# An eight-expert feed-forward layer: a loop of eight passes over token groups becomes one unrolled sequence

## The chip, the cores and the metric

The program runs on one core of a Trainium2 chip. The metric is the device time of one execution in microseconds (us). A core has a matrix engine (TensorE, PE in the profile; PEld are its weight loads), a vector engine (VectorE, DVE), a scalar engine (ScalarE, ACT), GpSimd (POOL) and SyncE (SP), which issues DMAs. The engines run their own instruction streams and meet at semaphores. PSUM is the memory that TensorE writes its results to, SBUF the working memory. Everything here is float32.

## The reference

The whole program is a stack of four attention-like layers and four feed-forward layers over a stream x of 4 x 1024 tokens with 128 features. Each adds its result to x. The change touches one of them, the feed-forward layer of the third block:

```python
x = x + L2_ffn(layernorm(x))

def L2_ffn(x):                                   # x: 4096 tokens x 128
    logits = x @ gate_w.T                        # 8 experts
    mult, sel = sparse_mixer_top2(logits, 0.01)  # two experts and two multipliers per token
    dense_w = zeros((T, 8)).at[rows, sel].set(mult)
    h1 = einsum('th,eih->eti', x, w1)            # 8 experts, 128 -> 256
    h3 = einsum('th,eih->eti', x, w3)
    act = silu(h1) * h3
    y = einsum('eti,ehi->eth', act, w2)          # 256 -> 128
    return einsum('eth,te->th', y, dense_w)

def sparse_mixer_top2(scores, eps):
    vals, idx = top_k(scores, 2)
    # for k = 1, 2: softmax over the scores s with (t_k - s) / max(|s|, t_k) <= 2 * eps
    # (for k = 2 without the first expert), and of it the value at idx_k
```

Every expert is computed for every token, and dense_w, zero for six of the eight experts, weights the results.

## The kernel before

The stream x lies in SBUF as X, [128, 32 tiles, 128]: 32 tiles of 128 tokens. The layer norm stage ahead of the layer writes its result turned, features on partitions, into XNT, [128, 32 * 128]. Stages follow one another; between two of them every engine waits at a barrier (`end_step`, which also has GpSimd clear the stage's semaphores).

`l2_ffn_stage` first loads and turns the weights (stages f2w0 to f2w2). Then comes stage f2s: `nc.Fori(0, TILES // G)` with G = 4, a loop in hardware of eight passes of four tiles each, with `end_step()` inside the loop. One pass has:

- ScalarE copies the pass's 512 columns of XNT into xs (L2279, with its table load), does two Exp for the routing (L2281, L2282) and 16 Tanh (L2287), from which silu is made.
- TensorE makes the logits of four tiles (L2293). Then for each expert e and each half k of its 256 hidden features it makes h1 (L2311) and h3 (L2313), products with 512 columns, and behind them the second product of the expert before, y(e-1) (L2302, eight products with 128 columns). In PSUM h1 and h3 have two buffers each and y has two.
- VectorE does the routing (L2323 to L2360), a chain of about 30 small instructions on 128x32 or 128x8 operands that ends with weight. After it, for each n = 2e + k, `hidden(n)` makes gated (L2365) and act (L2370). `gather(e-1)` adds weight times y(e-1) to acc (L2378 for the first expert, L2380 for the others), and at the end of the pass acc is added to X (L2392).

The waits that matter: TensorE may make h(n) when act(n-2) is done, and y(e) when act(2e+1) is done and y's buffer has been gathered. VectorE works in order, so that hidden(0) waits for the whole routing chain. `Chain` (called as `step`) makes an instruction signal a semaphore and VectorE wait for it, where the next one reads its result.

Each matmul in float32 stands in the trace as two instructions, so that L2302 has 16 for one expert. Two other stages have pieces of the same form: the last feed-forward layer's stage f3s makes the logits of 32 tiles (L3226) and a routing over 128x256 operands (L3280 to L3294), and the first feed-forward layer adds weighted products to X with one instruction a tile (L790). Neither is touched.

Of the kernel before, what the change touches and what calls it, by code (L numbers as in the profile page):

```python
# [18 lines left out]
U32 = mybir.dt.uint32  # L19
ACT = mybir.ActivationFunctionType  # L20
ALU = mybir.AluOpType
# [3 lines left out]
P = 128  # L25
# [2214 lines left out]
def l2_ffn_stage(nc, X, XNT, c, gate_w, w1, w2, w3):  # L2240


    with Stage(nc, "f2") as outer:
# [11 lines left out]
        with Stage(nc, "f2s") as st:  # L2255
            xs = st.sb("xs", [P, G * P])
            lg, size, gap, first, second, rest = (st.sb(n, [P, G, EXPERTS]) for n in
                                                  ("lg", "size", "gap", "first", "second", "rest"))
            ex1, ex2, lim1, lim2 = (st.sb(n, [P, G, EXPERTS]) for n in ("ex1", "ex2", "lim1", "lim2"))
            weight = st.sb("weight", [P, G, EXPERTS])  # L2260
            top = st.sb("top", [P, G, 8])
            at = st.sb("at", [P, G, 8], U32)
            atf = st.sb("atf", [P, G, 8])
            total, mult = (st.sb(n, [P, 2, G]) for n in ("total", "mult"))
# [3 lines left out]
            acc = st.sb("acc", [P, G, P])  # L2268
            logits = st.ps("logits", (P, G, EXPERTS))
            h1 = st.ps("h1", (P, 2, 512))  # L2270
            h3 = st.ps("h3", (P, 2, 512))
            y = st.ps("y", (P, 2, G, P))
            s = st.sems("xs_ready logits_ready shifted1 exps h1_ready h3_ready th_ready act_ready y_ready y_used "
                        "added chain")
            with nc.Fori(0, TILES // G) as i:
                with nc.Block(no_gpsimd_drain=True) as block:
                    @block.scalar
                    def _(a):
                        a.activation(xs[:], XNT[:, ds(i * G * P, G * P)], ACT.Copy).then_inc(s["xs_ready"], 1)  # L2279
                        a.wait_ge(s["shifted1"], 1)  # L2280
                        a.activation(ex1[:], ex1[:], ACT.Exp)  # L2281
                        a.activation(ex2[:], ex2[:], ACT.Exp).then_inc(s["exps"], 1)  # L2282
                        for n in range(2 * EXPERTS):
                            a.wait_ge(s["h1_ready"], n + 1)
                            if n >= 2:
                                a.wait_ge(s["act_ready"], n - 1)
                            a.activation(th[:, n % 2, :], h1[:, n % 2, :], ACT.Tanh, scale=0.5).then_inc(s["th_ready"], 1)  # L2287

                    @block.tensor
                    def _(pe):  # L2290
                        pe.wait_ge(s["xs_ready"], 1)
                        for j in range(G):
                            last = pe.matmul(logits[:, j, :], xs[:, j * P:(j + 1) * P], gT[:], start=True, stop=True)  # L2293
                        last.then_inc(s["logits_ready"], 1)

                        def second_product(e):
                            pe.wait_ge(s["act_ready"], 2 * e + 2)
                            if e >= 2:
                                pe.wait_ge(s["y_used"], e - 1)
                            for j in range(G):  # L2300
                                for k in range(2):
                                    last = pe.matmul(y[:, e % 2, j, :], act[:, e % 2, k, j * P:(j + 1) * P],  # L2302
                                                     w2T[:, e, k, :], start=(k == 0), stop=(k == 1))
                            last.then_inc(s["y_ready"], 1)

                        for e in range(EXPERTS):
                            for k in range(2):
                                n = 2 * e + k
                                if n >= 2:
                                    pe.wait_ge(s["act_ready"], n - 1)  # L2310
                                pe.matmul(h1[:, n % 2, :], w1T[:, e, k * P:(k + 1) * P], xs[:],  # L2311
                                          start=True, stop=True).then_inc(s["h1_ready"], 1)
                                pe.matmul(h3[:, n % 2, :], w3T[:, e, k * P:(k + 1) * P], xs[:],  # L2313
                                          start=True, stop=True).then_inc(s["h3_ready"], 1)
                            if e >= 1:
                                second_product(e - 1)
                        second_product(EXPERTS - 1)

                    @block.vector
                    def _(v):  # L2320
                        step = Chain(v, s["chain"])
                        v.wait_ge(s["logits_ready"], 1)
                        step(v.tensor_copy(lg[:], logits[:]))  # L2323
                        for j in range(G):
                            last = v.max(top[:, j, :], lg[:, j, :])
                        step(last)
                        for j in range(G):
                            last = v.max_index(at[:, j, :], top[:, j, :], lg[:, j, :])
                        step(last)
# [1127 lines left out]
```

## Time and profile before

| | |
|---|---|
| time, median of 3 runs | 8943.74 us (8923.92 to 8946.13) |
| time of the profiled execution | 8934.45 us |
| its span in the trace | 8932.6 us |
| stage f2s in the trace, its first ACT instruction to the first DVE instruction of the next stage | 6973.29 to 7408.45 |
| PE, DVE, ACT, POOL busy in the span | 83%, 66%, 46%, 33% |
| PE, DVE, ACT busy in f2s (6973 to 7408) | 372.5, 300.5, 92.7 us |

How to read it: all times of the trace are from the start of the span. The shares of the whole span say little on this change, since stages of quite different kinds stand in it; what counts is stage f2s, some 435 us. A row of the timeline has a start, a duration, the engine, the line in the kernel, what is written from what, and in brackets how long the engine had been idle and what ended that. The duration of one VectorE instruction is longer than the distance at which the next can start behind it, so that both are read: duration from the row, distance from two starts.

### The profile page before, as it was taken

What the parts mean: (1) busy time and instruction counts of PE and PEld (TensorE: products, weight loads), DVE (VectorE), ACT (ScalarE), POOL (GpSimd) and SP (SyncE); (2) the same over time, 40 slices, a digit from 0 to 9 for tenths busy, and PEclk for the clock granted to TensorE, in tenths of its full rate; (3) what the DMA queues carried; (4) which work ended last, traced back from release to release, by engine and by line L of the source; (5) the groups of instructions that cost most, each with busy time, mean ns of one, the idle gap of its engine ahead of it and who ended that gap; (6) DMA issues with size and microseconds to landing.
All of it is one profiled execution on the core that took longest, in us unless ns stands there. A gap on an engine that the chain in (4) does not pass through costs nothing. (4 is left out here: it accounts for less than half of the span.)

```text
span 8932.6 us, 296414 instructions
## 1 busy us (share of the span) xinstructions
PE 7426.1 (83%) x129614; PEld 5361.2 (60%) x129614; DVE 5916.2 (66%) x11095; ACT 4144.6 (46%) x6987; POOL 2904.6 (33%) x2116
## 2 busy tenths in 40 slices
PE   7998799999996987987987997997986784756666
PEld 3443588888885665665665665665664453645634
DVE  6664477777776876876866866866866667244266
ACT  3554244444444765765765765765752122111121
POOL 0110122222223753754754745745730000100000
PEclk9998699999998999999999999999998896555556
DMA  0000000000001221221212212212210000000000
GB/s 14 1 1 1 5 5 5 5 5 5 5 3 50 72 59 47 73 54 52 73 50 57 70 47 61 69 44 66 69 40 0 14 0 2 3 2 2 4 0 12
DMA packets 190372, 256.44 MB, mean 29 GB/s; under 512 B 58253, under 2 KB 84748, under 8 KB 188172
## 3 DMA queue, kind: packets, MB, share of 16 engines
q1 hardware_dynamic: 189068, 237.31, 10.0%
q8 instruction: 1031, 16.89, 0.8%
q14 instruction: 273, 2.24, 0.1%
HBM read 27.45 MB, written 2.10 MB: 3 GB/s over the span
## 5 line engine op out<-in xcount | busy, mean ns | idle before, releaser
L1758 PE MATMUL wa_front<-w_wqkv,wa_xsT 128*128 128x512 f32 x2400 | 1197.7, 622 | 53.2 <-PEq L66 24.4
L1680 POOL TENSOR_TENSOR XNT<-XNT 128x1024 f32<-128x1024 f32 x396 | 938.2, 2369 | 257.3 <-DVE XNT L1864 257.3
L1683 POOL TENSOR_TENSOR XNT<-XNT,wa_rnorm 128x1024 f32<-128x1024 f32 x396 | 754.2, 1904 | 438.1 <-DVE wa_rnorm L1872 438.1
L1861 DVE TENSOR_TENSOR XNT<-wa_front,w_scaled 128x1024 f32<-128x1024 f32 x396 | 472.4, 1193 | 381.2 <-ACT wa_sq L1699 279.8
L1758 PEld LDWEIGHTS wa_front<-w_wqkv,wa_xsT 128*128 128x128 f32 x2400 | 416.8, 194 | 387.5 <-issue 364.8
L1699 ACT ACTIVATE wa_sq<-wa_front 128x1024 f32<-128x1024 f32 x402 | 408.5, 1016 | 222.6 <-PE wa_front L1758 222.6
L1864 DVE TENSOR_TENSOR XNT<-wa_front,w_scaled 128x512 f32<-128x512 f32 x792 | 505.7, 680 | 0.0
L1877 DVE TENSOR_REDUCE wa_norm<-wa_sq 128x16 f32<-128x1024 f32 x396 | 478.7, 1209 | 0.0
L446 PE MATMUL a0h_ring<-a0h_QT,a0h_KT 32*128 32x512 f32 (+3 forms) x1536 | 449.0, 556 | 14.3 <-ACT a0h_E L564 10.4
L564 ACT ACTIVATE a0h_E<-a0h_ring 128x512 f32<-128x512 f32 (+1 forms) x640 | 320.6, 554 | 287.9 <-PE a0h_ring L446 285.8
L1764 PEld LDWEIGHTS wa_front<-consts,XNT 128*128 128x128 f32 x3168 | 358.7, 142 | 150.6 <-issue 74.5
L1764 PE MATMUL wa_front<-consts,XNT 128*128 128x128 f32 x3168 | 428.2, 278 | 17.8 <-issue 9.5
L1902 DVE TENSOR_TENSOR wa_o<-wa_back,wa_rtotal 128x1024 f32<-128x1024 f32 x198 | 242.5, 1225 | 256.0 <-PE wa_back L1820 256.0
L1846 PE MATMUL wa_back<-w_wo,wa_oT 128*128 128x128 f32 x3168 | 396.9, 280 | 6.7 <-ACT wa_oT L1744 6.7
L1686 POOL TENSOR_TENSOR wa_sc<-wa_sc,wa_smax 128x1024 f32<-128x1024 f32 x192 | 365.7, 1905 | 82.3 <-DVE wa_smax L1915 82.3
L1846 PEld LDWEIGHTS wa_back<-w_wo,wa_oT 128*128 128x128 f32 x3168 | 379.0, 196 | 9.1 <-ACT wa_oT L1744 9.1
L1820 PEld LDWEIGHTS wa_back<-wa_v_look,wa_pT 64*32 64x32 f32 x25344 | 267.2, 106 | 188.0 <-issue 179.1
L1348 POOL TENSOR_TENSOR a1s_Estrict<-a1s_E,a1s_sb 128x512 f32<-128x512 f32 x64 | 81.4, 1272 | 860.4 <-ACT a1s_E L1286 860.4
L1734 ACT ACTIVATE wa_v_all<-wa_front 128x1024 f32<-128x1024 f32 x198 | 203.0, 1025 | 323.1 <-PE wa_front L1758 323.1
L437 PE MATMUL a0h_slots<-a0h_KT,a0h_QT 32*128 32x512 f32 (+3 forms) x1536 | 341.8, 546 | 8.8 <-DVE a0h_part L643 4.2
L1820 PE MATMUL wa_back<-wa_v_look,wa_pT 64*32 64x64 f32 x25344 | 305.3, 228 | 34.4 <-issue 27.7
L2790 POOL TENSOR_TENSOR a3d_sb<-consts,a3x_nbeta 128x1024 f32<-128x1024 f32 x16 | 31.0, 1936 | 925.0 <-POOLq L66 925.0
(582 smaller groups left out, 18296.2 us busy)
## 6 DMA issues: line engine op xcount, KB each, us to landing
wa_v_look<-wa_v_all SPq DMA_DIRECT2D x1188, 128.0 KB, 2.3
wa_v_look<-wa_v_all SPq DMA_DIRECT2D x792, 64.0 KB, 2.0
w_wqkv<-in_L_ffn_Wqkv_dram SPq DMA_DIRECT2D x6, 1024.0 KB
w_wo<-in_L_ffn_Wo_dram SPq DMA_DIRECT2D x6, 512.0 KB
w_wqkv<-in_L_ffn_Wqkv_dram SPq DMA_DIRECT2D x12, 256.0 KB
f2w_raw<-in_L_ffn_w_dram SPq DMA_DIRECT2D x48, 64.0 KB, 1.9
out_dram<-X SPq DMA_DIRECT2D x1, 2048.0 KB, 8.7
w_w<-in_L_ffn_W_dram SPq DMA_DIRECT2D x6, 341.0 KB
```

Source lines behind the costliest of these rows:

```text
L446: last = pe.matmul(o[:, at:at + w], KT[rows, n % 3, kb * P:(kb + 1) * P], QT2[rows, k, 512 - w:512], start=True, stop=True)
L1680: g.tensor_tensor(rot[:, at], rot[:, at], part[:, at], ALU.add).then_inc(s[summed], 1)
L1683: g.tensor_tensor(rot[:, at], rot[:, at], spread(rnorm[:, at, :], HDW), ALU.mult).then_inc(s[done], 1)
L1686: g.tensor_tensor(sc[:], sc[:], spread(smax[:], LOOK), ALU.subtract).then_inc(s["less_max"], 1)
L1699: a.activation(sq[:, n].rearrange("p h d -> p (h d)"), two_banks(front, bank[n]), ACT.Square).then_inc(s[done], 1)
L1758: last = pe.matmul(front[:, first + i, :], xsT[:, slot, :], wqkv[:, (2 * n + i) * 512:(2 * n + i + 1) * 512], start=True, stop=True)
L1764: last = pe.transpose(front[:, first + i // 4, (i % 4) * P:(i % 4 + 1) * P], rot[:, n, 2 * i:2 * i + 2, :].rearrange("p h d -> p (h d)"), ...
L1820: last = pe.matmul(back[n * WINDOW:(n + 1) * WINDOW, p, i * HDW:(i + 1) * HDW], pT[r, i, n * WINDOW:(n + 1) * WINDOW], v_look[r, w, n, i * ...
L1846: last = pe.matmul(back[:, 0, 0:P], oT[:, i, :], wo[:, i, :], start=(i == 0), stop=(i == INNER // P - 1))
L1861: v.tensor_tensor(rot[:, n], src, cos, ALU.mult)
L1864: last = v.tensor_tensor(part[:, n, :, p0:p0 + 32], src[:, :, p1:p1 + 32], sin[:, :, p0:p0 + 32].broadcast_to([P, H, 32]), ALU.mult)
L1877: v.tensor_reduce(norm[:, n, :], sq[:, n], AX.X, ALU.add).then_inc(s[norm_in], 1)
```

## The change

The eight passes are gone. The routing is done once for all 32 tiles, on operands of 128x256, and then 64 pairs of (group of four tiles, expert) follow as one straight sequence in one block, written out by Python loops. Beside that: TensorE reads XNT itself, so that the copy xs goes; y has three buffers in PSUM where it had two; `gather` writes X directly and there is no acc; and `gather(i-2)` now stands between `hidden(2i)` and `hidden(2i+1)`, where `gather(e-1)` stood behind both. The comparisons for `first` and `second` were one instruction a tile each and are now one for all tiles.

```diff
-            xs = st.sb("xs", [P, G * P])
-            y = st.ps("y", (P, 2, G, P))
-            with nc.Fori(0, TILES // G) as i:
-                with nc.Block(no_gpsimd_drain=True) as block:
+            full = [P, TILES, EXPERTS]
+            y = st.ps("y", (P, 3, G, P))
+            logits = st.ps("logits", full)
+            work = [(g, e) for g in range(NG) for e in range(EXPERTS)]
+            with nc.Block(no_gpsimd_drain=True) as block:
...
-                        a.activation(xs[:], XNT[:, ds(i * G * P, G * P)], ACT.Copy).then_inc(s["xs_ready"], 1)
...
+                    for j in range(TILES):
+                        last = pe.matmul(logits[:, j, :], XNT[:, j * P:(j + 1) * P], gT[:], start=True, stop=True)
+                    last.then_inc(s["logits_ready"], 1)
+                    def second_product(i):
+                        g, e = work[i]
+                        pe.wait_ge(s["act_ready"], 2 * i + 2)
+                        if i >= 3:
+                            pe.wait_ge(s["y_used"], i - 2)
...
+                    for i, (g, e) in enumerate(work):
+                        xs = XNT[:, g * G * P:(g + 1) * G * P]
+                        for k in range(2):
+                            n = 2 * i + k
+                            if n >= 2:
+                                pe.wait_ge(s["act_ready"], n - 1)
...
+                        if i >= 1:
+                            second_product(i - 1)
+                    second_product(len(work) - 1)
...
-                        for j in range(G):
-                            v.tensor_scalar(first[:, j, :], c.count8, atf[:, j, 0:1], None, ALU.is_equal)
-                            last = v.tensor_scalar(second[:, j, :], c.count8, atf[:, j, 1:2], None, ALU.is_equal)
+                    v.tensor_tensor(first[:], count, atf[:, :, 0:1].broadcast_to(full), ALU.is_equal)
+                    step(v.tensor_tensor(second[:], count, atf[:, :, 1:2].broadcast_to(full), ALU.is_equal))
...
-                        def gather(e):
-                            v.wait_ge(s["y_ready"], e + 1)
...
-                        for e in range(EXPERTS):
-                            hidden(2 * e)
-                            hidden(2 * e + 1)
-                            if e >= 1:
-                                gather(e - 1)
-                        gather(EXPERTS - 1)
-                        v.tensor_tensor(X[:, ds(i * G, G), :], acc[:], X[:, ds(i * G, G), :], ALU.add).then_inc(s["added"], 1)
-                        v.wait_ge(s["added"], 1)
-                st.end_step()
+                    def gather(i):
+                        g, e = work[i]
+                        v.wait_ge(s["y_ready"], i + 1)
+                        if i >= 1:
+                            v.wait_ge(s["y_used"], i)
                         for j in range(G):
+                            t = g * G + j
+                            last = v.scalar_tensor_tensor(out=X[:, t, :], in0=y[:, i % 3, j, :], scalar=weight[:, t, e:e + 1],
+                                                          in1=X[:, t, :], op0=ALU.mult, op1=ALU.add)
+                        last.then_inc(s["y_used"], 1)
+                    for i in range(len(work)):
+                        hidden(2 * i)
+                        if i >= 2:
+                            gather(i - 2)
+                        hidden(2 * i + 1)
+                    gather(len(work) - 2)
+                    gather(len(work) - 1)
+                    v.wait_ge(s["y_used"], len(work))
+            st.end_step()
```

The instruction streams, first TensorE at the end of a pass. Before, two second products stand together and the loop's branch follows:

```order
L2311 MATMUL f2s_h<-f2s_xs,f_w1T 128x512
L2313 MATMUL f2s_h<-f2s_xs,f_w3T 128x512
L2311 MATMUL f2s_h<-f2s_xs,f_w1T 128x512
L2313 MATMUL f2s_h<-f2s_xs,f_w3T 128x512
L2302 MATMUL f2s_y<-f_w2T,f2s_act 128x128 x16
L2276 UNCONDITIONAL_BRANCH
L2275 REGISTER_ALU
L2275 COMPARE_AND_BRANCH
```

After, TensorE between any two experts, across the border of two groups too:

```order
L2299 MATMUL f2s_y<-f_w2T,f2s_act 128x128 x8
L2309 MATMUL f2s_h<-XNT,f_w1T 128x512
L2311 MATMUL f2s_h<-XNT,f_w3T 128x512
L2309 MATMUL f2s_h<-XNT,f_w1T 128x512
L2311 MATMUL f2s_h<-XNT,f_w3T 128x512
L2299 MATMUL f2s_y<-f_w2T,f2s_act 128x128 x8
```

The pair of second products now stands only at the very end of the stage.

VectorE in the midst of a pass, before: one expert's two `hidden`, and then the `gather` of the expert before it.

```order
L2378 TENSOR_SCALAR f2s_acc<-f2s_y,f2s_weight 128x128 x4
L2365 SCALAR_TENSOR_TENSOR f2s_gated<-f2s_th,f2s_h 128x512
L2370 SCALAR_TENSOR_TENSOR f2s_act<-f2s_h,f2s_gated 128x512
L2365 SCALAR_TENSOR_TENSOR f2s_gated<-f2s_th,f2s_h 128x512
L2370 SCALAR_TENSOR_TENSOR f2s_act<-f2s_h,f2s_gated 128x512
L2380 SCALAR_TENSOR_TENSOR f2s_acc<-f2s_y,f2s_weight,f2s_acc 128x128 x4
```

VectorE after, from the third pair on:

```order
L2362 SCALAR_TENSOR_TENSOR f2s_gated<-f2s_th,f2s_h 128x512
L2367 SCALAR_TENSOR_TENSOR f2s_act<-f2s_h,f2s_gated 128x512
L2378 SCALAR_TENSOR_TENSOR X<-f2s_y,f2s_weight,X 128x128 x4
L2362 SCALAR_TENSOR_TENSOR f2s_gated<-f2s_th,f2s_h 128x512
L2367 SCALAR_TENSOR_TENSOR f2s_act<-f2s_h,f2s_gated 128x512
```

The gather has moved from behind both halves to between them, and takes the y of two pairs ago.

## Rows read from the trace of the kernel before

**Rows 1.** Windows, second pass: length, busy time by engine, PE clock, DMA.

```profile
7027.00:7081.00 54.00, 45.62 (x200) 28.80 (x200) 37.56 (x107) 11.59 (x20) 0.00 (x0) 0.94 0.00 0
```

**Rows 2.** Timeline from the end of the second pass into the third (columns as above).

```profile
7078.09 1.13 DVE L2380 SCALAR_TENSOR_TENSOR f2s_acc<-f2s_y,f2s_weight,f2s_acc 128x128 f32<-128x128 f32 x4 [0.73 <-PE f2s_y L2302]
7079.37 0.69 DVE L2392 TENSOR_TENSOR X<-f2s_acc,X 128x512 f32 x1 [0.15 <-DVE f2s_acc L2380]
7081.34 1.28 ACT L2279 ACT_TABLE_LOAD   x1 [7.15 <-PEq L66]
7083.31 1.88 PE L2293 MATMUL f2s_logits<-f_gT,f2s_xs 128*128 128x8 f32 x8 [5.33 <-ACT f2s_xs L2279]
...
7085.23 0.19 DVE L2323 COPY f2s_lg<-f2s_logits 128x32 f32<-128x32 f32 x1 [5.16 <-PE f2s_logits L2293]
...
7091.95 0.69 DVE L2365 SCALAR_TENSOR_TENSOR f2s_gated<-f2s_th,f2s_h 128x512 f32<-128x512 f32 x1
...
7093.41 0.30 PEld L2311 LDWEIGHTS f2s_h<-f2s_xs,f_w1T 128*128 128x128 f32 x2 [3.61 <-DVE f2s_act L2370]
```

**Rows 3.** Timeline, experts in the midst of the second pass.

```profile
7039.39 1.13 PE L2311 MATMUL f2s_h<-f2s_xs,f_w1T 128*128 128x512 f32 x2 [3.07 <-DVE f2s_act L2370]
...
7048.15 1.95 PE L2302 MATMUL f2s_y<-f_w2T,f2s_act 128*128 128x128 f32 x16
...
7053.37 1.95 PE L2302 MATMUL f2s_y<-f_w2T,f2s_act 128*128 128x128 f32 x16
...
7070.81 1.02 PE L2311 MATMUL f2s_h<-f2s_xs,f_w1T 128*128 128x512 f32 x2
...
7072.58 0.69 DVE L2365 SCALAR_TENSOR_TENSOR f2s_gated<-f2s_th,f2s_h 128x512 f32<-128x512 f32 x1 [0.44 <-ACT f2s_th L2287]
...
7074.94 0.69 DVE L2370 SCALAR_TENSOR_TENSOR f2s_act<-f2s_h,f2s_gated 128x512 f32<-128x512 f32 x1
```

**Rows 4.** Timeline, first instruction of f2s and first VectorE work behind it.

```profile
6973.29 1.28 ACT L2279 ACT_TABLE_LOAD   x1 [43.99 <-PEq L66]
...
7408.45 1.65 DVE L134 BATCH_NORM_STATS2 ln_stats<-X 128x6 f32<-128x128 f32 x8 [1.12 <-PEq L66]
```

**Rows 5.** Timeline of the last feed-forward stage, logits and routing of 32 tiles.

```profile
8814.70 13.82 PE L3226 MATMUL f3s_logits<-f_rwT,XNT 128*128 128x8 f32 x64
...
8828.63 0.42 DVE L3280 TENSOR_TENSOR f3s_lg<-f3s_logits,f3s_bias 128x256 f32<-128x256 f32 x1 [13.66 <-PE f3s_logits L3226]
8829.09 2.27 DVE L3282 MAX8 f3s_top<-f3s_lg 128x8 f32<-128x8 f32 x32
...
8831.40 0.42 DVE L3284 TENSOR_TENSOR f3s_ex<-f3s_lg,f3s_top 128x256 f32<-128x256 f32 x1
8831.74 0.08 DVE L3286 MATCH_VALUE_LOAD f3s_at<-f3s_top,f3s_lg 128x8 f32 x1
...
8831.86 0.42 ACT L3266 ACTIVATE f3s_ex<-f3s_ex 128x256 f32<-128x256 f32 x1 [16.41 <-DVE f3s_ex L3284]
...
8836.21 0.29 DVE L3288 CAST f3s_atf<-f3s_at 128x256 f32<-128x256 uint32 x1
```

**Rows 6.** Groups by line and shape: a reciprocal of 128x64 in a later stage.

```profile
L2588 DVE RECIPROCAL a3x_rnorms<-a3p_sums 128x64 f32<-128x64 f32 x2 | 1.1, 553 | 2.2 <-ACT a3p_sums L2543 2.2
```

**Rows 7.** Instructions on X and on acc: durations in ns, least, median, most.

```profile
L2380 DVE SCALAR_TENSOR_TENSOR f2s_acc<-f2s_y,f2s_weight,f2s_acc x224: 340/342/352, 6996.1 to 7406.1; 128x128 f32<-128x128 f32 x112
L790 DVE SCALAR_TENSOR_TENSOR X<-f_y,f_gate,X x32: 341/343/352, 947.7 to 972.9; 128x128 f32<-128x128 f32 x32
```

**Rows 8.** Timeline, weight loads in the fifth pass after TensorE's wait.

```profile
7201.44 0.43 PEld L2311 LDWEIGHTS f2s_h<-f2s_xs,f_w1T 128*128 128x128 f32 x2 [3.01 <-DVE f2s_act L2370]
...
7204.94 0.20 PEld L2311 LDWEIGHTS f2s_h<-f2s_xs,f_w1T 128*128 128x128 f32 x1 [0.52 <-issue]
```

**Rows 9.** Windows in two other stages (columns as in Rows 1).

```profile
2000.00:2300.00 300.00, 289.57 (x6927) 250.10 (x6925) 228.57 (x447) 145.45 (x379) 83.34 (x92) 1.00 0.02 6
7600.00:7800.00 200.00, 146.36 (x4824) 133.61 (x4825) 51.12 (x113) 24.82 (x60) 19.60 (x12) 0.52 0.01 3
```

More of the change, by code:

```diff
@@ L2255, in l2_ffn_stage @@
         with Stage(nc, "f2s") as st:
-            xs = st.sb("xs", [P, G * P])
[L2257 to L2264, printed above, removed]
+            full = [P, TILES, EXPERTS]
+            NG = TILES // G
+            lg, size, gap, first, second, rest = (st.sb(n, full) for n in ("lg", "size", "gap", "first", "second", "rest"))
+            ex1, ex2, lim1, lim2 = (st.sb(n, full) for n in ("ex1", "ex2", "lim1", "lim2"))
+            weight = st.sb("weight", full)
+            top = st.sb("top", [P, TILES, 8])
+            at = st.sb("at", [P, TILES, 8], U32)
+            atf = st.sb("atf", [P, TILES, 8])
+            total, mult = (st.sb(n, [P, 2, TILES]) for n in ("total", "mult"))
             th = st.sb("th", [P, 2, 512])
```

163 lines of the change are left out of this document (68 added, 95 removed).

## Prediction

> **What bounds the kernel now.** I read three views in this order: the windows of stage f2s one pass at a time, then the timeline of one pass from its steady middle to its borders, then the same kind of work in other stages, where this one shows no price for it. Shares of the whole span are of no use here. f2s runs from 6973.29 to 7408.45 [rows 4], 435.16 us or 54.40 a pass. In a window of one pass TensorE is busy 45.62 of 54 us and VectorE 37.56 [rows 1], so neither engine is full. The timeline says why: there are two regimes.
>
> In the midst of a pass TensorE is the bound. Second products of two successive experts start at 7048.15 and 7053.37 [rows 3], so one expert takes 5.22 us; TensorE's rows follow one another without a gap that another engine ends. VectorE needs less: a `hidden` is two instructions of 0.69 at a distance of some 0.72, 1.41 us, and a `gather` 1.13 [rows 2, 3], which makes 2 x 1.41 + 1.13 = 3.95 us an expert.
>
> At the borders of a pass nothing is the bound, it is a chain across engines. From the third pass [rows 2]: the last gather ends at 7079.21, X is added at 7079.37, and the next pass's first instruction starts at 7081.34. There follow the table load and the copy xs, the logits at 7083.31, VectorE's first copy at 7085.23, and a routing of small instructions up to the first gated at 7091.95. TensorE, which has made h(0) and h(1) meanwhile, may go on at 7093.41, when act(0) is done. So one pass is 10.61 us (7081.34 to 7091.95), 1.46 to TensorE's restart, then the stream: in the second pass from the restart at 7039.39 to the end of the last gather at 7079.21, 39.82 [rows 2, 3], and 2.13 to the next pass. The sum is 54.02. Of the 39.82, seven experts are 36.54 and the drain at the end 3.28 (the last second product, and the last gather behind it).
>
> **The change part by part.** Eight times 54.02 is 432.2; the trace has 435.16, so about 3 us more lie in single passes. One cause is seen: in the fifth pass TensorE restarts at 7201.44 with weight loads 0.43 for two, the first at the faster rate again being at 7204.94 (0.20) [rows 8]. That is 3.5 us at the lower of the clock's two levels, 1.2 GHz, at which work takes twice as long, so 1.75 lost.
>
> After the change the stage is: logits, routing, restart, 63 further experts, drain, barrier. I price each from rows.
>
> Logits. Stage f3s has the same 64 instructions on 32 tiles: they start at 8814.70 and VectorE's first instruction behind them at 8828.63 [rows 5], 13.93 us, all at the low clock (13.82 for 64). I take the start at 6973.29, where the block's first instruction stands now [rows 4]; the table load and xs no longer stand ahead of TensorE, and ScalarE's table load for Exp has 30 us to hide in. If the clock were high it would be half, 7.0; above 13.93 nothing speaks for.
>
> Routing. In the order of the code: 14 instructions on 128x256 whose successor waits, at 0.46 each (8828.63 to 8829.09) = 6.44; 4 without a wait, at 0.34 (8831.40 to 8831.74) = 1.36; 32 MAX8 2.31 (8829.09 to 8831.40); 32 pairs of MAX_INDEX 4.47 (8831.74 to 8836.21) [all rows 5]. Three casts or tensor_scalar of 128x256 that are waited for, at the 0.29 of the cast and 0.04 for the wait, 0.99; two that aren't, about 0.20 each, 0.40, an estimate from the same row. One reciprocal of 128x64, 0.55 [rows 6] and 0.04. ScalarE's two Exp of 0.42 [rows 5] outlast rest and lim2 by about 0.2. Sum 16.76. By the shortest of these distances for all of it, it would be a little over 15; I keep 15 and 18 as its ends.
>
> Restart 1.46, as now. TensorE has then sat idle for some 11 us: logits end at about 6987, h(0) and h(1) take 7 us at the low clock, and act(0) comes at 7005.4. It restarts low, I take it. The fifth pass shows 1.75 lost after a shorter idle time [rows 8]; I take 2.0. The ends are 0 (the restart in rows 2, two loads in 0.30, is at the high level) and 3.4 (h(2) and h(3) wholly at the low one).
>
> Stream. 63 experts follow, 63 x 5.22 = 328.86, and the drain, 3.28. Nothing else is in TensorE's order: at a group's border only the slice of XNT changes. The cover that must hold is VectorE's. With h(2i) at 0, gated starts at 1.77 (7070.81 to 7072.58) [rows 3]; `hidden(2i)` ends at 3.18, the gather, whose y has been ready since 0, at 4.31, and `hidden(2i+1)` at 5.72. In the old order it ended at 4.82 (7074.94 + 0.69). h(2i+3) needs it, at 5.22 + 1.72 = 6.94. So 1.2 us are left of the cover where there were 2.1; the moved gather costs nothing. The third y buffer gives room that the stream doesn't need. Gathering into X costs what gathering into acc does: 342 against 343 ns [rows 7]. No DMA and no SP or POOL work is moved.
>
> Barrier 1.12 to the next stage [rows 4]; the add of X (0.69) is gone.
>
> Sum: 13.93 + 16.76 + 1.46 + 2.0 + 328.86 + 3.28 + 1.12 = 367.4, against 435.2: 67.8 us less. In words: seven borders of 54.02 - 41.76 = 12.26 us go (86), so do the 3 us by which single passes are longer and 1.0 at the end of the stage (2.13 to 1.12), and the one head that is left grows from 10.61 to 30.69 and restarts 2.0 slower. Against the profiled execution's 8934.45 that gives 8866.7. That run lies 9.3 below the median shown, 8943.74, from which it would be 8876.0. I forecast the middle, 8871.
>
> **A rule weighed.** The traffic of instructions is the one resource this trace can't price. The rows of a dense straight stage show 6927 matmuls with their loads in 300 us, 23 pairs a us, with TensorE busy 289.57 [rows 9]; the new stream needs 24 pairs in 5.22 us, 4.6 a us. By that row straight code comes in fast enough, at no cost. The Trainium skill (Runtime: NRT & Kernel Launch, section on instruction fetch mechanics) says that fetching ahead is purely sequential and a taken branch can stall it, which speaks for the change, and that straight code pays at block crossings, mostly hidden, which speaks against it. By the first the borders removed would include such a stall; it is in the 54.02 already, so the sum stays.
>
> **Rivals.** Times are on the same base as 8871.
>
> A, VectorE becomes the bound or its cover is too thin: the gather between the two halves makes each act(2i+1) late. For it: VectorE's order is longer before the act that TensorE needs. Against: the 1.2 us above. If the period went from 5.22 to the 5.72 at which VectorE ends, 63 x 0.5 = 31 us come back: 8903.
>
> B, straight code comes in late. If each expert lost what a pass's start loses before its first work, about 1.3 us (the 2.13 between passes less the 0.84 for the add), 64 x 1.3 = 83 come back: 8954, no change. Against: rows 9.
>
> C, the other side, slower: the clock stays at 1.2 GHz. The place is the restart after the long idle time. A later stage runs at 0.52 of full clock though TensorE is busy 146 of 200 us [rows 9], so that being busy most of the time doesn't bring the clock back there. If the whole stream ran so, 63 x 5.22 = 329 us are added: 9200. It decides from where more than 136 us of the stream are at the low level (each costs half of itself, and 67.8 are to be lost). Against: in the fifth pass the level was back 3.5 us after the restart [rows 8], and the dense stage holds 1.00 [rows 9]. The Trainium skill (TensorE: Matmul & The Clock Gate, section on oscillation) says that waits between bursts throttle the clock again and again and unbroken bursts keep it; the fast middle of each pass agrees with it, and it is against C.
>
> D, a better case: the logits or the restart run at the high level. Up to 7.0 + 2.0 less: 8862.
>
> That the change doesn't do what it says would be a border that survives at each eighth expert. The order of instructions has none, so it has no chance of its own.
>
> **How the numbers follow.** The forecast has 0.82, A 0.08, D 0.04, B 0.03, C 0.03. About 0.3%, 27 us, is what can be told from no change here. Forecast, A and D are faster by more than that: 0.94. B is within it: 0.03. C is slower: 0.03. The range: the known ends are -9 (D), +1.4 for the restart, +/-1.5 for the routing, and the runs of before spread by 22 us (8923.92 to 8946.13), which is more than all of these. From 8871 I go down to 8848 and up to 8903, where A lies.
>
> **What would show it.** Right: f2s of some 367 us; one row of 64 logits of about 13.8 us; the routing some 17 us long; second products 5.22 us apart from the first to the last, also at every eighth; VectorE idle only before gated, never before a gather; clock 1.00 from a few us behind the restart. The stages after it unchanged. Wrong: TensorE waiting for act in the stream (A), gaps named issue or PEq with nothing else late (B), a clock of 0.5 in windows of the stream (C), or stages elsewhere that take another time than before, which I have taken as fixed.

## The result, and the profile after

The changed kernel takes 8871.58 us (median of four runs, 8862.99 to 8875.53), the kernel before 8944.93 us beside it (8923.92 to 8946.68). The ratio is 0.9924, with a 95% interval of 0.9909 to 0.9939: 0.8% faster. The forecast was 8871.

The profiled execution took 8875.03 us, its span is 8873.3. First the timeline of the head of stage f2s, the same columns as [rows 2]: start, duration, engine, line, what is written from what, and in brackets the idle time before it and what ended that.

```profile
6978.07 1.28 ACT L2278 ACT_TABLE_LOAD   x1 [43.79 <-PEq L66]
6978.11 13.79 PE L2289 MATMUL f2s_logits<-f_gT,XNT 128*128 128x8 f32 x64 [1.29 <-PEq L66]
...
6991.94 0.42 DVE L2321 COPY f2s_lg<-f2s_logits 128x256 f32<-128x256 f32 x1 [14.79 <-PE f2s_logits L2289]
6992.40 2.27 DVE L2323 MAX8 f2s_top<-f2s_lg 128x8 f32<-128x8 f32 x32
...
7008.61 0.69 DVE L2362 SCALAR_TENSOR_TENSOR f2s_gated<-f2s_th,f2s_h 128x512 f32<-128x512 f32 x1
...
7010.07 0.50 PEld L2309 LDWEIGHTS f2s_h<-XNT,f_w1T 128*128 128x128 f32 x2 [13.94 <-DVE f2s_act L2367]
...
7016.20 1.95 PE L2299 MATMUL f2s_y<-f_w2T,f2s_act 128*128 128x128 f32 x16
```

The head is a straight chain: the logits end, VectorE copies them 13.87 us after the stage began, routing runs 16.67 us to the first gated at 7008.61, and TensorE restarts 1.46 later after 13.94 us of idle time. The price of MAX8, 2.27, is that of [rows 5].

Then the end of the stage, the last regular gather and the drain:

```profile
7322.44 0.69 DVE L2362 SCALAR_TENSOR_TENSOR f2s_gated<-f2s_th,f2s_h 128x512 f32<-128x512 f32 x1 [1.46 <-ACT f2s_th L2284]
...
7323.77 1.11 DVE L2378 SCALAR_TENSOR_TENSOR X<-f2s_y,f2s_weight,X 128x128 f32<-128x128 f32 x4
...
7325.51 0.69 DVE L2367 SCALAR_TENSOR_TENSOR f2s_act<-f2s_h,f2s_gated 128x512 f32<-128x512 f32 x1
...
7339.84 4.13 PE L2299 MATMUL f2s_y<-f_w2T,f2s_act 128*128 128x128 f32 x32
7341.92 1.86 PEld L2299 LDWEIGHTS f2s_y<-f_w2T,f2s_act 128*128 128x128 f32 x16 [0.32 <-DVE f2s_act L2367]
...
7344.01 1.13 DVE L2378 SCALAR_TENSOR_TENSOR X<-f2s_y,f2s_weight,X 128x128 f32<-128x128 f32 x4 [1.05 <-PE f2s_y L2299]
...
7346.10 1.64 DVE L134 BATCH_NORM_STATS2 ln_stats<-X 128x6 f32<-128x128 f32 x8 [0.96 <-PEq L66]
```

From y(0) at 7016.20 to y(62) at 7339.84 are 323.64 us, 62 times 5.22 to the hundredth: no border of a group is left in it. The stage is 6978.07 to 7346.10, 368.0 us, where it was 435.16 [rows 4].

The waits of the stage (what waited, for what; us in total, times, longest):

```profile
DVE f2s_gated L2362 <- ACT f2s_th L2284: 93.9, 64, 2.1
...
PEld f2s_h L2309 <- DVE f2s_act L2367: 13.9, 1, 13.9
...
DVE X L2378 <- PE f2s_y L2299: 1.1, 1, 1.1
...
PEld f2s_y L2299 <- DVE f2s_act L2367: 0.3, 1, 0.3
```

TensorE waits for act in the head, and once more, 0.3 us, in the drain (7341.92), but never in the stream between them. VectorE waits for a y once, at the very end; in between its idle time is ahead of gated. The windows, in the columns of [rows 1], show the clock:

```profile
7004.00:7010.00 6.00, 0.00 (x0) 0.00 (x0) 5.52 (x15) 1.69 (x4) 0.00 (x0) 0.50 0.00 0
7010.00:7100.00 90.00, 89.92 (x395) 55.75 (x396) 61.48 (x132) 20.32 (x34) 0.00 (x0) 0.97 0.00 1
7100.00:7200.00 100.00, 100.00 (x465) 63.65 (x465) 71.02 (x155) 22.71 (x38) 0.00 (x0) 1.00 0.00 1
```

The granted clock is at the lower level at the end of the routing and at 1.00 in the stream, where TensorE is busy 100 of 100 us.

The whole span is only 59.3 us shorter, though the stage is 67.1 shorter: the work ahead of the stage took 4.8 us longer in this execution (it ends at 6978.07, not 6973.29) and that behind it some 3.1. Nothing in these layers was changed, and over all the profiled executions here, those of the variants below among them, the stage begins anywhere between 6959.3 and 6983.6. So the stage's length, not the span, is what the experiments are compared by. It is read from one profiled execution of each kernel.

### The profile page after: what moved, and what is told of

It reads as the page before. It is cut to its first block and busy times, and to the rows that moved or that the text cites. A ratio compares the mean times of both kernels' runs of the same rounds, so it can differ in the third digit from the quotient of the medians.

```text
span 8873.3 us, 295885 instructions
## 1 busy us (share of the span) xinstructions
PE 7414.0 (84%) x129614; PEld 5360.5 (60%) x129614; DVE 5866.2 (66%) x10871; ACT 4129.7 (47%) x6958; POOL 2904.2 (33%) x2116
## 5 line engine op out<-in xcount | busy, mean ns | idle before, releaser
L606 POOL TENSOR_SCALAR_AFFINE_SELECT a0h_E<-a0h_E 128x512 f32<-128x512 f32 x128 | 80.0, 637 | 754.7 <-ACT a0h_E L564 754.7
```

## The experiments

Each is a variant of the changed kernel. The first four were timed with the kernel before at 8948.02 us (8929.73 to 8955.67), the next three had one execution each beside 8934.07, the last three were timed with the kernel before at 8933.48 (8915.21 to 8941.52). The time is a median of ten runs for the kept loop, of two for the old place of the gather, and of four or five for the others. "Stage" is from the first instruction of f2s to the first VectorE instruction of the next stage.

| variant | time, us | ratio to before, 95% | stage, us |
|---|---|---|---|
| loop kept, routing hoisted | 8922.43 | 0.9974 (0.9962 to 0.9985) | 414.3 |
| unrolled, routing by group | 8883.67 | 0.9931 (0.9911 to 0.9950) | 373.9 |
| old place of the gather, two y buffers | 8869.38 | 0.9919 (0.9899 to 0.9939) | 364.5 |
| routing spread | 8864.38 | 0.9914 (0.9898 to 0.9931) | 353.6 |
| products in the wait | 8855.27 | one execution | 363.0 |
| one extra add a pair | 8878.66 | one execution | 368.1 |
| three extra adds a pair | 8921.19 | one execution | 405.3 |
| spread, logits in time | 8848.66 | 0.9900 (0.9884 to 0.9917) | 349.4 |
| spread, logits apart | 8845.94 | 0.9903 (0.9889 to 0.9916) | 347.2 |
| the changed kernel again | 8878.00 | 0.9938 (0.9924 to 0.9951) | 368.0 |

### Which half of the change gave the time

**The loop kept, the routing hoisted out of it.**

```diff
             st.end_step()
+            with nc.Fori(0, TILES // G) as i:
+                with nc.Block(no_gpsimd_drain=True) as block:
...
+                        step(v.tensor_copy(wg[:], weight[:, ds(i * G, G), :]))
...
+                st.end_step()
```

Ahead of the first `end_step` stand logits and routing of 32 tiles as in the changed kernel. The loop has the pass of before without logits, routing and Exp; wg is the pass's part of weight.

> One part of the change alone: the routing is done once for all 32 tiles, ahead of the loop, and the loop of eight passes with its barrier, its table load, its copy xs, acc and two y buffers stays. Theory (the gain is the border of a pass, of which routing is only one of two parallel strands): the routing ahead costs 30.7 us and a barrier of about 1.3; a pass still has 2.1 us of barrier, 1.3 of table load and 0.6 of xs, and then h(0) and h(1), about 6.8 us at the low clock, so that TensorE restarts some 8 us after the pass begins where it was 12.1. 8 x 3.9 = 31 us less against 32 more: stage f2s stays at about 436 us, the time at before's 8945, +/- 10. Rival (the small routing instructions carry the gain): eight chains of 7 to 10 us gone for one of 17, stage at about 385 us, the time near 8895.

Measured: 414.3 us, 22 below the theory and 29 above the rival. Timeline, the border of two passes:

```profile
7042.41 0.63 ACT L2336 ACTIVATE f2s_xs<-XNT 128x512 f32 x1 [7.15 <-PEq L66]
...
7043.09 0.30 PEld L2361 LDWEIGHTS f2s_h<-f2s_xs,f_w1T 128*128 128x128 f32 x2 [4.23 <-ACT f2s_xs L2336]
...
7090.17 0.63 ACT L2336 ACTIVATE f2s_xs<-XNT 128x512 f32 x1 [7.15 <-PEq L66]
```

A pass is 47.76 us, by the copies xs at 7042.41 and 7090.17; the first pass, from 6993.94, is the only longer one, 48.47. That is 6.26 less than the 54.02 of before, since not only logits and routing leave it but the table load of [rows 2], 1.3 us, too. A border still costs 47.76 - 41.76 = 6.0 us. The new head takes 31.7 us (6962.27 to 6993.94), so hoisting alone saves 20.9. Unrolling saves the further 46.3: seven borders are 42 of it, the rest is at the first pass's start and the stage's end.

That Exp and Tanh no longer alternate isn't what removes the table load. The next variant has Exp and Tanh by turns at each of eight groups and only one table load in the stage, at its start, like every unrolled kernel here. In the kernel before it stood at the head of the loop's body and so ran in each of the eight passes; here it stands ahead of the loop.

**Unrolled, the routing left at each group.** The operations are those of the changed kernel on four tiles at a time (`queue[g]`), and TensorE makes a group's eight logits products straight ahead of its first h.

```diff
             for i, (g, e) in enumerate(work):
+                if e == 0:
+                    plan += [("route", op) for op in queue[g]]
...
                 plan.append(("hidden", 2 * i))
```

> The unrolled sequence with no barrier, but logits and routing made per group of four tiles (128x32 operands) at the head of each group, in VectorE's order. Theory: the head shrinks from 30.7 to about 9 us; at each of the seven later borders VectorE is late by the routing of about 6.7 us less the 2.0 us of cover, 4.7, and TensorE makes four logits, 0.85: 7 x 5.6 = 39. Stage f2s 368 - 22 + 39 = about 385 us, the time 17 above after, near 8889. Rival (unrolling and dropping the barrier are the whole gain, the batch of 32 doesn't matter): stage at 346 to 368, time 8850 to 8872. Second rival (the clock falls in each of the seven waits): 2 us more in each, 399.

Measured: 373.9 us, 11 below the theory. TensorE at a border, and behind its wait at the next one:

```profile
7026.90 0.96 PE L2348 MATMUL f2s_logits<-f_gT,XNT 128*128 128x8 f32 x8
...
7031.23 1.95 PE L2358 MATMUL f2s_y<-f_w2T,f2s_act 128*128 128x128 f32 x16
7035.19 1.77 PE L2372 MATMUL f2s_h<-XNT,f_w1T 128*128 128x512 f32 x2 [2.02 <-DVE f2s_act L2407]
7036.76 1.91 PE L2374 MATMUL f2s_h<-XNT,f_w3T 128*128 128x512 f32 x2
...
7040.43 1.83 PE L2358 MATMUL f2s_y<-f_w2T,f2s_act 128*128 128x128 f32 x15
...
7081.84 1.12 PE L2372 MATMUL f2s_h<-XNT,f_w1T 128*128 128x512 f32 x2 [2.03 <-DVE f2s_act L2407]
```

Without a barrier TensorE has h(2i), h(2i+1) and y(i-1), 5.2 us, to run beside the routing of four tiles, and waits for 2.0 only. In three of the seven borders that wait leaves the clock at 1.00 and the border costs 3.8 us, 0.9 of it the logits. In the other four, the first one above among them, a stretch of products at up to twice their length follows and the border costs 4.9 to 5.0; so the second rival's clock loss came in four waits, with 1.1 each and not 2. Seven borders cost 31.2 us in all. y(0) comes after 12.8 us here and after 38.1 in the changed kernel: 25.4 less. The difference is the 5.9 measured. So given the unrolling, "for all tiles at once" is worth 6 us, 9% of the gain in the stage; in the loop, with its barriers kept, it is worth 20.9. The unrolling, and with it the end of barrier, copy, table load and refill, is nearly all of the gain in this order.

### Does the new gather matter, and is VectorE's cover real

**The old place of the gather, two y buffers.**

```diff
                 hidden(2 * i)
-                if i >= 2:
-                    gather(i - 2)
                 hidden(2 * i + 1)
+                if i >= 1:
+                    gather(i - 1)
```

> The changed kernel with one part undone: the gather of pair i-1 behind both hidden products, and two y buffers. Theory (the third buffer and the moved gather give nothing): stage f2s within 0.5 us of the 368.0 of after, second products 5.22 us apart. Rival (the move of the gather or the third buffer was needed at group borders or in the stream): a period above 5.22, each 0.1 us in it being 6.3 in the stage.

Measured: 364.5, with second products 5.22 apart throughout. VectorE's waits and the head:

```profile
DVE f2s_gated L2362 <- ACT f2s_th L2284: 43.6, 126, 1.5
DVE X L2378 <- PE f2s_y L2299: 38.5, 64, 0.7
```

```profile
6971.19 11.29 PEld L2289 LDWEIGHTS f2s_logits<-f_gT,XNT 128*128 128x128 f32 x64 [1.55 <-issue]
...
7000.76 0.50 PEld L2309 LDWEIGHTS f2s_h<-XNT,f_w1T 128*128 128x128 f32 x2 [12.93 <-DVE f2s_act L2367]
```

VectorE now waits for each y (64 times), and it costs nothing. Of the 3.5 us below the forecast 3.1 are not the gather's: the 64 logits took 11.3 us here, 13.8 in the changed kernel, because the clock was still high in a part of them (granted 1.00 from 6971 to 6973, 0.50 from 6975 on), and y(0) came 5.44 behind the restart, not 6.13. The last 0.4 are the gather's. From y(62) to the next stage it is 5.86 here and 6.26 in the changed kernel, where the gather between the last two halves makes act(127) late and TensorE waits 0.32 us with y(63) (7341.92), which it doesn't here. So in the stream the moved gather and the third buffer earn nothing that these runs can show, and in the drain the moved gather costs 0.4.

**Extra work on VectorE.** One, and then three adds of 128x512 a pair, two of the three between the halves.

```diff
                             gather(i - 2)
+                        step(v.tensor_tensor(spare[:, 0, :], spare[:, 1, :], spare[:, 1, :], ALU.add))
+                        step(v.tensor_tensor(spare[:, 0, :], spare[:, 1, :], spare[:, 1, :], ALU.add))
                         hidden(2 * i + 1)
+                        step(v.tensor_tensor(spare[:, 0, :], spare[:, 1, :], spare[:, 1, :], ALU.add))
```

This is the edit with three adds; with one, only the last of them stands there.

> The changed kernel with one VectorE add of 128x512 (0.72 us with its wait) more in each pair, behind hidden(2i+1). Theory (TensorE is the bound and VectorE has 1.2 to 1.5 us to spare in a pair): period stays 5.22, stage 368 +/- 1.5. Rival (VectorE's order is already what sets the period): each 0.72 adds 45 us.

Measured: 368.1, no loss, with y after y at 5.22 throughout.

> As the kernel with one extra add, but three of them in a pair, two between gather and hidden(2i+1) and one behind: 2.16 us, which is more than the idle 1.46 us before gated that the trace of after shows in a pair. Theory: VectorE becomes the bound, period 5.22 + 0.70 = 5.9, stage 368 + 44 = 412. Rival (there is more room than the idle time shows, since the waits overlap): less than 20 us more.

Measured: 405.3 for some 412. Of the difference 3.1 lie in the head (y(0) after 35.1 us for 38.1), most of the rest in the period. A pair takes 5.85 us and VectorE is busy 97.08 of 100:

```profile
7150.35 1.12 PE L2310 MATMUL f2s_h<-XNT,f_w1T 128*128 128x512 f32 x2 [0.36 <-DVE f2s_act L2369]
...
7152.26 1.12 DVE L2380 SCALAR_TENSOR_TENSOR X<-f2s_y,f2s_weight,X 128x128 f32<-128x128 f32 x4
7153.30 0.68 DVE L2388 TENSOR_TENSOR f2s_spare<-f2s_spare 128x512 f32<-128x512 f32 x1
7154.01 0.69 DVE L2389 TENSOR_TENSOR f2s_spare<-f2s_spare 128x512 f32<-128x512 f32 x1
7154.74 0.69 DVE L2364 SCALAR_TENSOR_TENSOR f2s_gated<-f2s_th,f2s_h 128x512 f32<-128x512 f32 x1
7155.46 0.69 DVE L2369 SCALAR_TENSOR_TENSOR f2s_act<-f2s_h,f2s_gated 128x512 f32<-128x512 f32 x1
7156.07 0.68 DVE L2391 TENSOR_TENSOR f2s_spare<-f2s_spare 128x512 f32<-128x512 f32 x1
```

By the starts, a gather takes 1.04 of VectorE (7152.26 to 7153.30), gated 0.72 and act, which nothing on VectorE waits for, 0.61. A pair needs 1.04 + 2 x 1.33 = 3.70, and leaves 1.52 of 5.22; three adds are 2.15, and 3.70 + 2.15 is the 5.85 measured. The changed kernel's idle time of 1.46 ahead of gated (7322.44) says the same.

### The head

**Products in the wait.** Twelve products of 128x512 into the third buffer of y, which y(2) is the first to use, ahead of TensorE's wait for act(0).

```diff
+                if i == 1:
+                    for _ in range(12):
+                        pe.matmul(y[:, 2].rearrange("p j d -> p (j d)"), w1T[:, 0, 0:P], xs, start=True, stop=True)
```

> The changed kernel with twelve products of 128x512 added between h(1) and h(2), written to the third y buffer and overwritten later; they fill 10 of the 13 us that TensorE waits for act(0). Theory (the clock falls in that wait and costs 2.6 us after it): weight loads behind the restart at 0.19 instead of 0.34 us, the first second product 3.54 us behind h(2) instead of 6.13, stage f2s 365.4. Rival (the slow start is not the clock but the restart itself): still 6.13, stage 368.0.

Measured: 363.0, 5.0 below the changed kernel. PE and its loads:

```profile
6959.47 11.27 PEld L2289 LDWEIGHTS f2s_logits<-f_gT,XNT 128*128 128x128 f32 x64 [1.55 <-issue]
...
6976.76 10.46 PE L2307 MATMUL f2s_y<-XNT,f_w1T 128*128 128x512 f32 x24
...
6989.02 0.30 PEld L2312 LDWEIGHTS f2s_h<-XNT,f_w1T 128*128 128x128 f32 x2 [2.63 <-DVE f2s_act L2370]
```

h(2) restarts after 2.63 us of idle time in place of 13.94, with loads of 0.30 in place of 0.50, and y(0) is there 3.54 later in place of 6.13. The granted clock is 1.00 in the window of 4 us behind this restart. In the changed kernel it is 0.50 from 7010 to 7014 and 1.00 only from 7016 on. So 2.6 us were the clock's. The other 2.4 are the logits again, 11.3 for 13.8.

**The routing spread over VectorE's free time.** Four rounds, of one, one, two and four groups. Some 3 us of the first round stand ahead of the first gated and its rest behind `hidden(0)` and `hidden(1)`; of the others VectorE does about 1 us of work a pair. (`spend(t, n)` puts the next routing instructions worth t us into VectorE's list.)

```diff
+            rounds = [(0, G), (G, 2 * G), (2 * G, 4 * G), (4 * G, NG * G)]
...
+            spend(3.0, 0)
             for i, (g, e) in enumerate(work):
                 plan.append(("hidden", 2 * i))
...
                 plan.append(("hidden", 2 * i + 1))
+                spend(1.6 if i < 2 else 1.05, 2 * i + 2)
...
+            logits_at = {0: [0], 2: [1], 12: [2, 3], 26: [4, 5, 6, 7]}
```

> The unrolled sequence with the routing taken out of TensorE's way: logits and routing in four rounds (group 0, group 1, groups 2 and 3, groups 4 to 7), whose instructions are put singly into the time that VectorE has to spare between the hidden products. Theory (after the change only the head of 30.7 us is left to gain, and VectorE has 1.2 to 1.5 us free in each pair): h(0) starts after 1.7 us, two low-clock products cost about 3.4 more, the other logits 5 to 6 us of TensorE's time at the high clock, no wait for act: stage about 348 us, 20 below after, time near 8852. Rival (VectorE has no such room, the instructions put in push act back): the stream's period rises above 5.22 in the first 30 pairs, stage 360 or more.

Measured: 353.6, 5.6 above the forecast. y(0) is there 11.9 us after the start. The loss is in two places; the first, TensorE and VectorE:

```profile
6993.86 1.85 PE L2363 MATMUL f2s_logits<-f_gT,XNT 128*128 128x8 f32 x16
6997.55 2.07 PE L2387 MATMUL f2s_h<-XNT,f_w1T 128*128 128x512 f32 x2 [1.83 <-DVE f2s_act L2422]
```

```profile
6995.82 0.23 DVE L2287 COPY f2s_lg<-f2s_logits 128x64 f32<-128x64 f32 x1 [6.20 <-PE f2s_logits L2363]
6996.08 0.69 DVE L2417 SCALAR_TENSOR_TENSOR f2s_gated<-f2s_th,f2s_h 128x512 f32<-128x512 f32 x1
```

VectorE works in order, and the copy of the logits stood in its list one pair before TensorE issued them. It sat 6.20 us with two gated products ready behind it, TensorE waited 1.83, and its next products ran at half rate (2.07 for 1.02). The second place is the 32 logits of groups 4 to 7: the y behind them comes 10.49 us after the y ahead of them, where 5.22 + 4 x 0.89 = 8.8 are work.

**The logits one pair earlier, and then each group's apart.** The first variant's `logits_at` is computed in its code; here it stands with its values.

```diff
-            logits_at = {0: [0], 2: [1], 12: [2, 3], 26: [4, 5, 6, 7]}
+            logits_at = {0: [0], 2: [1], 10: [2, 3], 26: [4, 5, 6, 7]}                              # in time
+            logits_at = {0: [0], 2: [1], 8: [2], 10: [3], 20: [4], 22: [5], 24: [6], 26: [7]}       # apart
```

> As the kernel with the routing spread in four rounds, but the 16 logits products of groups 2 and 3 stand one pair earlier on TensorE, straight before the first products of the pair that VectorE turns to behind its copy of them (n = 10 in place of 12). In the earlier run VectorE's copy of these logits stood ahead of hidden(10) in its list while TensorE issued them only ahead of h(12), so VectorE stood 6.20 us with two gated products queued behind, TensorE waited 1.83 us for act, and four products then ran at the low clock: y(4) to y(5) took 11.81 us where 5.22 + 1.7 are work. Theory 1 (that wait is what brought the clock down): both go, y to y across these logits is 6.9, and the stage is 353.6 - 4.9 = 348.7. Theory 2 (long runs of 8-column products bring the clock down by themselves, as the 32 of groups 4 to 7 did with no wait behind them: 10.49 us where 5.22 + 3.5 are work): across the 16 logits it stays some 1.5 above 6.9, and the stage is 350.3. Either way the time is near 8864.4 - 4 = 8860.

Measured: 349.4. From the start of one y to that of the next, across the 16 logits, it is 7.00 us: full rate, no loss. Across the 32:

```profile
7053.25 1.95 PE L2377 MATMUL f2s_y<-f_w2T,f2s_act 128*128 128x128 f32 x16
7055.04 4.37 PE L2367 MATMUL f2s_logits<-f_gT,XNT 128*128 128x8 f32 x32
7059.26 2.06 PE L2391 MATMUL f2s_h<-XNT,f_w1T 128*128 128x512 f32 x2
...
7065.40 1.95 PE L2377 MATMUL f2s_y<-f_w2T,f2s_act 128*128 128x128 f32 x16
```

The window over them has TensorE busy 11.00 of 11.00 us at a granted clock of 0.69:

```profile
7055.00:7066.00 11.00, 11.00 (x48) 7.42 (x48) 4.31 (x16) 1.19 (x2) 0.00 (x0) 0.69 0.00 0
```

There is no idle time here, and still the first products behind the logits take 2.06 us for 1.02, as do the two groups of products that follow them (1.91 and 1.90). From y to y it is 12.15 where 5.22 + 4 x 0.89 = 8.8 are work: 3.4 lost. So theory 1 holds for the first place and theory 2 for the second. The stage's 349.4 alone couldn't tell the two apart: the first logits ran at the high level here (1.03 us for 1.84), and y(0) came 10.2 us after the start in place of 11.9.

> As the one before it, but each group's 8 logits products stand alone, ahead of eight different pairs (n = 0, 2, 8, 10, 20, 22, 24, 26), so no run of 8-column products is longer than 0.9 us. Theory 2 (long runs of them bring the clock down): no low-clock stretch is left behind the head, every y to y with logits between is 5.22 + 0.86 = 6.08, and the stage is 353.6 - 4.9 - 1.8 = 346.9. Theory 1 (only waits do): the 1.8 us behind the last logits is still there, and the stage is 348.7.

Measured: 347.2, near the 346.9 of theory 2. The stream, at a group's logits:

```profile
6994.81 1.95 PE L2373 MATMUL f2s_y<-f_w2T,f2s_act 128*128 128x128 f32 x16
6996.59 0.96 PE L2363 MATMUL f2s_logits<-f_gT,XNT 128*128 128x8 f32 x8
6997.40 1.10 PE L2387 MATMUL f2s_h<-XNT,f_w1T 128*128 128x512 f32 x2
```

All six distances with logits in them are 6.11 or 6.12, all others 5.22. The stage is 12.0 to y(0), 62 x 5.22 + 6 x 0.89 = 329.0 of stream, and 6.3 of drain and barrier.

> The changed kernel itself beside the two, for their difference on one chip: 8871.6 by the earlier runs, its stage 368. Against it the two should be 15 to 21 us shorter if what the stage loses reaches the time.

Measured: stage 368.0, the same as in the first execution, and 8878.00 us (8868.76 to 8878.82). The variant with logits apart has 8845.94 (8832.72 to 8854.16), and the intervals of the two ratios don't meet: it beats both kernels. Its stage is 20.8 us shorter; the medians differ by 32, and the cause of the 11 more stays open: nothing outside the stage differs in the two programs. In the two profiled executions the stage begins 6.2 us apart (6972.37 and 6978.58).

## Why the prediction was right

| term | forecast | measured |
|---|---|---|
| logits to VectorE's copy | 13.93 | 13.87 |
| routing | 16.76 | 16.67 |
| restart | 1.46 | 1.46 |
| loss at the low clock | 2.0 | 2.6 |
| stream | 328.86 | 328.87 (63 x 5.22) |
| drain | 3.28 | 3.6 |
| barrier | 1.12 | 0.96 |
| stage | 367.4 | 368.0 |

The first three and the stream are read off the rows above. The drain is the rest: 7345.14, the end of the last gather, less the restart (7010.07), the loss and the stream.

- **Logits and routing.** Pricing them by the last stage's rows [rows 5], in distances between starts, held to 0.1 us each. The low clock of the logits was right for this execution but isn't a constant: in three of the profiled variants (old place of the gather, products in the wait, three extra adds) the same 64 products took 11.2 to 11.4. That is a part of rival D, and 2.4 us of its 7.
- **The restart at the low clock** was the most mis-sized term, 2.0 for 2.6. It was taken from a restart behind a 3 us wait [rows 8], in a pass that lost 1.7. Behind waits of 13.9 to 14.1 us it was 2.5 to 2.6 in three executions, and behind waits of 12.9 us 1.9 and 2.0 in two; whether the length of the wait decides stays open. That it is the clock, the granted clock of 0.50 and the filled wait both show. The idle time was 13.9 us for the forecast 11, since the clock came back during h(0) and h(1), which took 5.2 us and not 7.
- **The drain** was put 0.3 too low, 3.28 for 3.6. It was read off a pass in the old order, and the forecast weighed the moved gather in the stream alone. In the drain no h covers the act that it delays, which costs the 0.4 found above.
- **Borders.** The forecast said that seven borders of 12.26 go. None is left in the stream, and the kept loop divides them: 6.3 go with logits, routing and table load, 6.0 with the loop's barrier, copy, drain and refill. Most of this goes without the batch of 32 as well: with the routing left at each group, but no barrier, a border costs 4.5 on average. The "3 us in single passes" are there too: from the y(6) of one pass to the y(0) of the next, five borders of before take 22.7 us and two take 24.39 and 24.18, 3.2 more in all.
- **VectorE's cover (rival A).** Refuted. The forecast 3.95 us a pair was too high; by starts it is 3.70, since the gather takes 1.04 and act 0.61. `hidden(2i+1)` ends 5.45 behind h(2i)'s start (7320.75 to 7326.20), not 5.72, and 1.5 before h(2i+3) starts, for the forecast 1.2. One more add costs nothing, three make VectorE the bound.
- **Straight code (rival B).** Refuted. Over the stage the DMA queues of before and of after show:

```profile
q8 instruction: 2, 0.03, 0.0%
q14 instruction: 1, 0.01, 0.0%
```

```profile
q8 instruction: 13, 0.21, 0.2%
q14 instruction: 8, 0.07, 0.1%
```

  There are 21 packets of instructions where there were 3, and 62 distances of 5.22 without one longer. The Trainium skill (Runtime: NRT & Kernel Launch, section on instruction fetch mechanics) says that block crossings of straight code are mostly hidden; in this stream the trace agrees, wholly hidden.
- **The clock (rival C).** Refuted: 1.00 from 7100 on, and 0.97 in the 90 us that hold the restart.
- **Stages elsewhere.** They weren't fixed, as the forecast took them to be. They took some 8 us more in this execution, and the reference to the median of before happened to absorb that, which was luck: 8866.7 was worked out against the profiled execution, 8875.03 was measured for the profiled one, and 8871 was the middle between 8866.7 and 8876.0. The stage was forecast to 0.6 us, the whole time no better than the spread of its other layers allows.

Three forecasts of the experiments failed in a step of their own. For the kept loop (22 us) the theory left the 1.3 us of table load in each pass and priced h(0) and h(1) at 6.8 us; h(2) started 5.2 behind h(0). For the routing by group (11 us) it made VectorE 4.7 late at a border, which was 2.9 where the clock held (3.8 less 0.9 of logits), and let the head shrink by 22 where it shrank by 25.4. For the spread routing (5.6 us) it took the work as free wherever VectorE has time, and left out that a wait for another engine in an in-order list holds all that is behind it.

## What to carry to other kernels

Where every pass of a loop ends in a chain across engines, price the border apart from the middle. Here a border was 12.3 us against 5.2 for an expert, and unrolling, which removed the barrier, was worth far more than batching the small work: once the stream ran without barriers, one batch ahead of it and eight small ones inside it differed by 6 us. Spreading it into VectorE's free time gained a further 21. When small work is spread into a stream, put its producer on the other engine at least as early as its consumer's place in the list, and break up long runs of tiny matmuls. Reordering that costs nothing in the stream can still cost in the drain, where nothing covers it.

## What the runs showed of the hardware beside this

- A run of 32 logits products (8 columns each, 3.6 to 4.4 us) was followed by products at the rate of 1.2 GHz, where it had been that of 2.4 GHz, with no idle time in TensorE's rows; it cost 3.4 us, and in the kernel with the routing spread 1.7 (10.49 from y to y); 16 or 8 of them didn't.
- The same 64 logits took 13.8 us in both executions of the changed kernel and in two variants, and 11.2 to 11.4 in three: the level on entry to the stage differs. Where they took less, the granted clock was 1.00 in the first 2 us and 0.50 some 4 us after the start, while TensorE was busy all the time; where they took 13.8 it was 0.50 from the start. The first eight logits took 1.84 in three variants and 1.03 in the one with the logits in time.
- A wait of TensorE of about 2 us didn't settle the clock. One of 1.8 us was followed by products at twice their length (2.07 for 1.02). Of seven of 2.0 us, at the borders of the routing by group, four were followed by a low stretch that cost 1.1 us, and three left the granted clock at 1.00. Waits of 0.36 every pair with three extra adds left the clock at 1.00.
- Eight logits products in the stream cost 0.89 us at the high level. At the low one 64 of them took 13.8, 1.7 for eight.
- All unrolled kernels have one table load (1.28 us) in the stage though Exp and Tanh alternate in some; the loop of before had it in each of its eight passes.
- Layers that nobody changed placed the start of the stage between 6959.3 and 6983.6 us, a spread of 24 us, about as much as the 27 us within which the forecast counted a kernel as unchanged.
